# One attention, expert and state-space layer: first operand's rows by three transfers, and the last batches' routing in another order

## What is computed

```python
x = x + attention(layernorm(x))      # 16 heads of 8, rotary, causal softmax
x = x + experts(layernorm(x))        # 8 experts of 512, the 2 best of each token
x = x + state_space(layernorm(x))    # gates, FFT convolution, a feed-forward part
x = x + experts(layernorm(x))        # the same experts again
```

## Time and profile before

| | |
|---|---|
| median of 3 runs | 688.79 us (686.36 to 688.85) |
| profiled execution | 690.77 us, span 689.0 us |
| mean granted TensorE clock | 0.868 of full |
| TensorE busy | 516.5 us (75%) |
| VectorE busy | 377.3 us (55%) |
| ScalarE busy | 253.2 us (37%) |
| GpSimd busy | 318.0 us (46%) |

### The profile page before, as it was taken

One profiled execution on the slowest core, in us unless ns is written; L12 is line 12 of the kernel. 1 busy time (PEld: TensorE's weight loads), 2 busy tenths in 40 slices (PEclk: granted clock), 3 DMA queues, 4 the chain that ended last, 5 costly groups with the idle time before them and its releaser, 6 DMA issues. The chain is left out here.

```text
span 689.0 us, 12192 instructions
## 1 busy us (share of the span) xinstructions
PE 516.5 (75%) x3527; PEld 355.4 (52%) x3528; DVE 377.3 (55%) x1247; ACT 253.2 (37%) x519; POOL 318.0 (46%) x373
## 2 busy tenths in 40 slices
PE   3994699999999867577992089899679610699970
PEld 1442344554655336576992044545447510699970
DVE  3864546888887744452442548741745771244433
ACT  1312345767766733232446133101023110344432
POOL 1454035965254762364543485145321476155553
PEclk9997757999999989898997589999879855699995
DMA  6154103214322114233435000000000013122216
GB/s 176 47 183 147 49 1 84 76 48 128 109 68 64 55 42 120 59 105 103 110 110 142 1 0 0 1 0 1 0 1 0 21 54 81 44 71 71 70 50 183
DMA packets 45992, 46.11 MB, mean 67 GB/s; under 512 B 8133, under 2 KB 39424, under 8 KB 45792
## 3 DMA queue, kind: packets, MB, share of 16 engines
q1 hardware_dynamic: 37440, 31.48, 16.7%
q0 software_dynamic: 4544, 9.35, 4.1%
q10 hardware_dynamic: 3952, 4.59, 2.0%
HBM read 31.68 MB, written 15.12 MB: 68 GB/s over the span
## 5 line engine op out<-in xcount | busy, mean ns | idle before, releaser
L1282 ACT ACTIVATE store<-ps 128x512 f32<-128x512 f32 x160 | 91.5, 595 | 55.4 <-PE ps L850 55.1
L1070 DVE TENSOR_REDUCE at_mx<-ps 128x1 f32<-128x512 f32 (+1 forms) x128 | 74.1, 617 | 29.8 <-PE ps L837 29.5
L835 PE MATMUL ps<-at_hats 72*128 72x512 bf16 (+3 forms) x256 | 75.2, 331 | 11.8 <-DVE at_mx L1070 10.1
L1367 POOL TENSOR_SCALAR_AFFINE_SELECT store<-store 128x512 f32<-128x512 f32 x64 | 39.0, 635 | 72.5 <-ACT store L1282 72.4
L850 PE MATMUL ps<-at_hats 74*128 74x512 bf16 (+3 forms) x256 | 66.9, 328 | 6.5 <-DMA at_hats<-at_mT 6.5
L461 POOL DMA_INDIRECT expert_rows<-r_rows,r_sloti x64 | 62.2, 972 | 19.1 <-issue 18.1
L597 POOL DMA_INDIRECT expert_results<-at_vall x39 | 37.5, 961 | 54.6 <-DVE at_vall L539 32.7
L597 POOL DMA_INDIRECT expert_results<-moe_y,moe_targeti x39 | 37.4, 958 | 49.0 <-DVE moe_y L539 46.0
L837 PE MATMUL ps<-c_mask_q_bf,c_ident_bf 128*128 128x128 bf16 x256 | 54.1, 236 | 0.0
L867 PE MATMUL ps<-store,at_vext 128*32 128x128 f32 (+3 forms) x512 | 51.7, 482 | 0.5 <-ACT at_oT_more L1250 0.5
L571 PE MATMUL ps<-at_vall,at_hats 128*128 128x128 f32 x312 | 44.7, 290 | 7.1 <-issue 4.1
(11 more groups left out here) (313 smaller groups left out, 1048.6 us busy)
## 6 DMA issues: line engine op xcount, KB each, us to landing
at_hats<-parts SPq DMA_DIRECT2D x32, 288.0 KB
moe_w<-moe_w_dram SPq DMA_DIRECT2D x8, 512.0 KB, 6.0
store<-ssm_tables_dram SPq DMA_DIRECT2D x35, 86.0 KB
at_vall<-expert_rows SPq DMA_DIRECT2D x39, 64.5 KB
moe_xg<-expert_rows SPq DMA_DIRECT2D x39, 64.5 KB
at_hats<-expert_results SPq DMA_DIRECT2D x8, 256.0 KB, 5.1
moe_ytok<-expert_results SPq DMA_DIRECT2D x8, 256.0 KB, 4.9
parts<-store ACTq DMA_DIRECT2D x12, 128.0 KB
```

The source lines that it names most:

```text
L835: pe.matmul(bankA(n)[:, col:col + (t + 1) * P], hatq[0:MROW, slot, h, t * P:(t + 1) * P], hatk[0:MROW, slot, h, 0:(t + 1) * P], start=True ...
L1070: m = dve.tensor_reduce(mx[:, u % 2, t, h:h + 1], bankA(n)[:, 0:(t + 1) * P], AX.X, ALU.max)
L1282: act.activation(pt[:, u % 2, j // 2, S * (j % 2):S * (j % 2 + 1)], bankB(n), ACT.Exp).then_inc(s_e, 1)
L1367: pool.affine_select(out=own, in_=own, compare_op=ALU.is_ge, fill=0.0, base=0, pattern=[[0, HG], [1, P]], channel_multiplier=-1).then_inc( ...
```

## The change

The load of `hatq` in `load_hats` is three transfers of 24 partitions each in place of one with a repeated source; a slot's semaphore then counts 64 per use. In the last units of attention and behind it, steps of the routing stand at other places; group 2's logits are read by VectorE in place of ScalarE. No arithmetic is changed.

```diff
--- before.py
+++ after.py
@@ -788,17 +788,17 @@
         ROUTE_PE = {(8, 0): ("transposes", 0), (8, 3): ("logits", 0), (11, 3): ("ranks", 0),
                     (12, 0): ("transposes", 1), (12, 3): ("logits", 1), (14, 3): ("ranks", 1), (15, 0): ("totals", 0),
-                    (15, 2): ("transposes", 2), (15, 4): ("logits", 2)}
+                    (15, 1): ("transposes", 2), (15, 3): ("logits", 2)}
         ROUTE_ACT = {(8, 1): ("copy_T", 0), (8, 2): ("copy_rows", 0), (8, 4): ("copy_logits", 0),
-                     (12, 1): ("copy_T", 1), (12, 2): ("copy_rows", 1), (12, 4): ("copy_logits", 1), (15, 3): ("copy_T", 2)}
+                     (12, 1): ("copy_T", 1), (12, 2): ("copy_rows", 1), (12, 4): ("copy_logits", 1), (15, 2): ("copy_T", 2)}
         ROUTE_DVE = {(6, 4): ("moments", 0, halves[0]), (7, 0): ("moments", 0, halves[1]),
                      (9, 2): ("choice", 0, 0), (10, 2): ("choice", 0, 1), (10, 3): ("choice", 0, 2),
                      (11, 1): ("choice", 0, 3), (11, 4): ("slots", 0),
                      (10, 4): ("moments", 1, halves[0]), (11, 0): ("moments", 1, halves[1]),
-                     (13, 2): ("choice", 1, 0), (14, 0): ("choice", 1, 1), (14, 1): ("choice", 1, 2),
-                     (14, 2): ("choice", 1, 3), (14, 3): ("moments", 2, range(GT)), (14, 4): ("slots", 1),
-                     (15, 0): ("plan", 0), (15, 1): ("rescale", 2)}
-        SCATTERS = {12: (0, 0), 13: (0, 1), 14: (1, 0), 15: (1, 1)}
+                     (13, 2): ("choice", 1, 0), (13, 4): ("choice", 1, 1), (14, 0): ("choice", 1, 2),
+                     (14, 1): ("choice", 1, 3), (14, 3): ("moments", 2, range(GT)), (14, 4): ("slots", 1),
+                     (15, 0): ("rescale", 2), (15, 1): ("plan", 0)}
+        SCATTERS = {11: (0, 0), 12: (0, 1), 14: (1, 0)}
         @block.tensor
         def _(pe):
@@ -828,7 +828,7 @@
                 n, slot = NA * u + k, u % SLOTS
                 if k == 0:
-                    pe.wait_ge(s_hat[slot], 32 * (u // SLOTS + 1))
+                    pe.wait_ge(s_hat[slot], 64 * (u // SLOTS + 1))
                 if n >= 3:
                     pe.wait_ge(s_ar, n - 2)
                 for h, t, col in A_CHUNKS[k]:
@@ -978,28 +978,28 @@
             for t in range(TPB):
                 pv(UNITS - 1, t)
-            tail(B - 1, 0)
-            tail(B - 1, 1)
             router.ranks(pe, 2)
-            tail(B - 1, 2)
-            tail(B - 1, 3)
+            for r in range(4):
+                tail(B - 1, r)
             expert(0)
             tail(B - 1, 4)
             expert(1)
             tail(B - 1, 5)
             router.totals(pe, 1)
-            for i in range(2, 6):
-                expert(i)
+            expert(2)
+            expert(3)
             pe.wait_ge(router.s_off, 4)
             router.transposes(pe, 3)
-            expert(6)
+            expert(4)
             router.logits(pe, 3)
-            for i in range(7, 10):
+            for i in range(5, 8):
                 expert(i)
             router.ranks(pe, 3)
+            expert(8)
+            expert(9)
+            router.totals(pe, 2)
             expert(10)
             expert(11)
-            router.totals(pe, 2)
             over_slot_tiles(pe, lambda i, u: experts.tensor(pe, i, u), begin=12)
         @block.vector
@@ -1148,13 +1148,11 @@
             def expert(i):
                 experts.vector(dve, i, i % 4)
-            router.first_choice(dve, 2)
-            router.second_choice(dve, 2)
+            router.choose(dve, 2)
             tail(B - 1, 0)
-            tail(B - 1, 1)
             router.slots(dve, 2)
-            tail(B - 1, 2)
-            tail(B - 1, 3)
+            for r in range(1, 4):
+                tail(B - 1, r)
             expert(0)
             tail(B - 1, 4)
             expert(1)
@@ -1163,22 +1161,21 @@
             router.moments(dve, 3)
             expert(2)
             router.plan(dve, 1)
+            router.normalize(dve, 3)
             expert(3)
             expert(4)
-            router.normalize(dve, 3)
             expert(5)
-            expert(6)
             router.read_logits(dve, 3)
             router.first_choice(dve, 3)
+            expert(6)
+            router.second_choice(dve, 3)
             expert(7)
-            router.second_choice(dve, 3)
             expert(8)
+            router.slots(dve, 3)
             expert(9)
-            router.slots(dve, 3)
             expert(10)
-            expert(11)
             router.plan(dve, 2)
-            over_slot_tiles(dve, lambda i, u: experts.vector(dve, i, u), begin=12)
+            over_slot_tiles(dve, lambda i, u: experts.vector(dve, i, u), begin=11)
             router.gates(dve)
             turns.vector_setup(dve)
             experts.add_second(dve)
@@ -1295,16 +1292,15 @@
             def expert(i):
                 experts.scalar(act, i, i % 4)
-            router.copy_logits(act, 2)
             o_copy(UNITS - 1)
             router.copy_rows(act, 2)
-            for i in range(6):
+            for i in range(4):
                 expert(i)
             router.copy_T(act, 3)
-            expert(6)
+            expert(4)
             router.copy_rows(act, 3)
-            expert(7)
-            expert(8)
+            for i in range(5, 9):
+                expert(i)
             over_slot_tiles(act, lambda i, u: experts.scalar(act, i, u), begin=9)
             router.gap_exponentials(act)
             turns.scalar_setup(act)
@@ -1354,6 +1350,10 @@
             for u in range(UNITS):
                 if u in (6, 10, 14):
                     add_attention(u // GROUPS - 1)
+                if u == 14:
+                    router.inverse_root(pool, 2)
+                if u == 15:
+                    router.scatter(pool, 1, 1)
                 if u in (7, 11):
                     router.inverse_root(pool, u // GROUPS - 1)
                     router.rescale(pool, u // GROUPS - 1)
@@ -1371,8 +1371,6 @@
                 if u == turns.PARTS:
                     pool.wait_ge(turns.s_made, 1)
                     router.numbers(pool)
-                if u == 14:
-                    router.inverse_root(pool, 2)
                 if u in SCATTERS:
                     router.scatter(pool, *SCATTERS[u])
@@ -1380,20 +1378,18 @@
                 experts.results(pool, i, i % 4)
             router.scatter(pool, 2, 0)
-            expert(4)
-            expert(5)
             router.scatter(pool, 2, 1)
             router.inverse_root(pool, 3)
-            for i in range(6, 12):
+            for i in range(4, 10):
                 expert(i)
             router.scatter(pool, 3, 0, range(0, 2))
+            expert(10)
+            router.scatter(pool, 3, 0, range(2, 4))
+            expert(11)
+            router.scatter(pool, 3, 1, range(0, 2))
             expert(12)
-            router.scatter(pool, 3, 0, range(2, 4))
-            expert(13)
-            router.scatter(pool, 3, 1, range(0, 2))
-            expert(14)
             router.scatter(pool, 3, 1, range(2, 4))
-            over_slot_tiles(pool, lambda i, u: experts.results(pool, i, u), NSLOT + 4, begin=15)
+            over_slot_tiles(pool, lambda i, u: experts.results(pool, i, u), NSLOT + 4, begin=13)
             experts.add_first(pool)
         @block.sync
@@ -1408,7 +1404,8 @@
                 heads = slice(HG * g, HG * (g + 1))
                 q = parts_dram[b, 0].rearrange("i p t -> (i p) t").rearrange("(n h) t -> n h t", h=NH)[:, heads, :]
                 k = parts_dram[b, 1].rearrange("i p t -> (i p) t").rearrange("(n h) t -> n h t", h=NH)[:, heads, :]
-                sp.dma_start(hatq[0:MROW, slot, :, :], bc(q, 3, 0)).then_inc(s_hat[slot], 16)
+                for r in range(3):
+                    sp.dma_start(hatq[3 * DH * r:3 * DH * (r + 1), slot, :, :], q).then_inc(s_hat[slot], 16)
                 sp.dma_start(hatk[0:MROW, slot, :, :], bc(k, 3, 1)).then_inc(s_hat[slot], 16)
             def max_row(u):
```

## The result

The changed kernel takes 652.25 us (median of 4 runs, 651.33 to 653.21), the kernel before 687.58 in the runs beside it: a ratio of 0.9495 with a 95% interval of 0.9451 to 0.9539, 35.3 us less. The profiled execution took 653.21 with a span of 651.5, 37.5 less than before. The forecast of 645 was 7 us too low, within its range of 636 to 663.

What follows compares the result with a forecast made beforehand. The prediction blamed query loads confined to three transfer engines, the stalls and low TensorE clock that follow, and late routing. Gains summed to 44.8 us: 690.77 to 646.0, taken as 645 for the median, range 636 to 663.

Steps and rivals of the forecast that it cites:

- maxima begin: Start of the kernel: VectorE's row maxima begin earlier because batch 1's store no longer holds ScalarE; gain 9.0 us.
- two units of maxima: Start: the maxima of two units take 12.6 us at full clock, where they ran from 59.71 to 75.03; gain 2.7 us.
- row maxima land: First unit: unit 0's row maxima land before TensorE wants them at 63, so its wait goes; gain 5.7 us.
- clock in the first units: First attention units: without the two stalls TensorE keeps its full clock; gain 12.5 us, bounds 0 and 14.
- end of attention: Last units to first expert tile: the rows' 4.42 us wait goes, selects come 2.1 us later; net gain 1.4 us.
- first tile to tile 17: Expert tiles: group 3's transposes come earlier, gain 10.5 us, and the stretch to the first pad shortens, gain 3 us.
- The cause: Loads at the start: the query load, factor 3 outermost, keeps three of 16 transfer engines busy at 26 GB/s each.
- splitting gains nothing: Rival for the loads: three transfers share the same engines, so only the routing's 15 us is left: 676 us; chance 0.05.
- the store of batch 1 would land by about 46: Start: with loads at 279 GB/s and issuing the slower side, this store lands before ScalarE is free at 47.93.
- the clock stays low anyway: Rival for the first units: TensorE still gets half speed, so 12.5 and 2.7 us are lost: 660 us; chance 0.15.
- The third stage: Expert tiles up to tile 17: gains of 10.5 us at group 3's transposes and 3 us to the first pad.
- signs listed for a right forecast: Across the profile: ScalarE's store wait at most 2 us, maxima near 51, exponentials near 64, tile 17 some 46 us behind first tile.

## Why the prediction was right, and where it was off

Each step of the sum, predicted and as the profiles of before and after have it (positive is a gain). The first exponentials before, on which two steps rest, are here:

```profile
80.84 1.28 ACT L1282 ACT_TABLE_LOAD   x1 [10.38 <-PE ps L850]
```

| Step | predicted | measured | from |
|---|---|---|---|
| maxima begin | 9.0 | 5.2 | 59.71 to 54.53 |
| two units of maxima | 2.7 | 0.9 | 15.3 to 14.4 |
| row maxima land | 5.7 | 6.3 | end of the maxima to first exponentials: 5.8 to -0.5 |
| clock in the first units | 12.5 | 12.8 | 42.4 to 29.6, exponentials to unit 4 |
| end of attention | 1.4 | 1.2 | 135.6 to 134.4, unit 4 to first tile |
| first tile to tile 17 | 13.5 | 12.1 | 59.1 to 47.0 |
| behind tile 17 | 0 | -1.0 | 371.1 to 372.1 |
| **sum** | **44.8** | **37.5** | spans 689.0 to 651.5 |

The sum came to 646.0 for the profiled execution; less the 2 us between it and the median that is 644, and I took 645.

**The cause** was right: three engines carried the query load. Two kernels show it from both sides, the single transfer with its repeat inside (same gain) and the one with 23 rows (one engine). The rival that splitting gains nothing was right in a narrower sense: the split gained nothing, the outermost size all.

**The step that failed** is "the store of batch 1 would land by about 46": its term of 9.0 was sized by 279 GB/s and by the thought that issuing is then the slower side. Issuing was faster than I had it (9.2 us for units 0 to 3, not 12), the transfers slower: 167 to 237 GB/s between 36 and 52, so the store landed at 52.4. That the loads ahead of it hold it is shown by the run that issued two units' loads and not four: there it landed 5.0 us behind its issue, and not 11.8. In all profiles with fast loads these are 5.0 to 5.6 us behind two units' loads (three kernels) and 9.6 to 11.8 behind four (five kernels). The short rest of a stall, some 3.4 us in which TensorE was idle (51.8 to 55.3), still cost the clock from 57 to 61, and with it most of the 2.7. These two steps are 5.6 of the 7.3 us that the sum was too large by. In the three kernels whose maxima began at 51.95 to 53.30 the clock held, so part of these 5.6 us is the late start of this profile. That the store lands well behind 46 holds in all five.

**The clock** was the largest term of the sum and the best hit: from the first exponentials to unit 4 are 29.6 us in every profile in which the clock was full there, with fast loads and in the one with slow loads and 36 unread matmuls, and 42.4 where it fell at the start of the stretch and came back at 112. Its rival, that the clock stays low anyway, lost; the profile in which the clock fell after 2.19 us of idling shows how little was needed for it to come true.

**The end of attention** went as described: later selects and no wait for rows. Its size, 1.2 us, can't be told from the spread: kernels with the old order of the routing have 134.9 to 136.2 us there, those with the new one 133.2 to 137.9, wherever the scatter stands. **The third stage** came 12.1 us nearer, 8.9 of it at the transposes (10.5 predicted), 2.5 from there to the first pad (3 predicted), and 0.7 from the pads on, which I had as unchanged. This one is well clear of the spread: 46.4 to 48.3 us from the first tile to tile 17 with the new order of all engines, 59.1 to 61.2 with the old.

Of the signs listed for a right forecast, three are missed: ScalarE's wait for the store is 7.2 us where under 2 was asked, the maxima begin at 54.53 and not near 51, and the first exponentials come at 68.42 and not near 64. Of those for a wrong one, the clock of 0.50 is there up to 60.5, just inside the stretch named, and the new wait for selects is 5.59 us, just under the 6 named. All but the last point at the step that failed.

## What to carry to other kernels

Look at the share of the transfer engines while someone waits for a transfer: here a plateau at 3/16 was a load whose outermost size is 3, and one at 1/16 a load of 23 rows. Then try a size with a large common factor outermost on both sides, as 24 and 72 were here, by repeating inside or by several transfers. What a stall costs isn't its length alone: here 15 us of stalls took 13 us more through the clock. So shortening a stall may bring little until it is nearly gone, as the profile with 2.19 us left shows. A small transfer on which an engine waits can be held long by bulk loads ahead of it in the queue: 8 KB waited for 5.7, 16.3 and 50.3 us here. So moving the bulk earlier for one wait must be checked against the next.

## What the runs showed that I had not expected

- Full use of TensorE didn't bring its clock back soon. With 10 and 6 unread matmuls, 2.19 us of idling were followed by a fall at 81, and the clock stayed at 0.50 until 112 at a busy share of 1.00. That is 31 us behind the stall, as before the change. With batch 1's store ahead of unit 2 it took 21 us behind a stall of 16.3 us with slow loads, and 16 us behind one of 4.3 us with fast loads; with 23 rows 16 us behind one of 50.3 us. After a stall of 3.4 us in the changed kernel, followed by the maxima's matmuls, it was back 3.4 us after its fall. What sets this isn't shown.
- Twelve engines didn't carry four times what three did. Three moved 78 GB/s, 26 each; twelve 167 to 251 in stretches with a share of 0.7 to 0.86, 13 to 21 GB/s for each engine's worth of share, beside the stores.
- Profiles of the same, untouched work differ: from the load of tile 17 to the end 371 to 376 us. Edits worth 1 to 4 us where they act could not be told from none in the total.
